# Attention: a step's weighing is issued behind all four scores and maxima of the next step

## The chip, the cores and the metric

The kernel runs on one core of one Trainium2 chip. The metric is the device time of one execution in microseconds (us); the time before is the median of three runs. The engines are TensorE (PE in the profile; PEld are its weight loads), VectorE (DVE), ScalarE (ACT), GpSimd (POOL) and SyncE (SP, which here only issues DMAs).

## The reference

A stack of blocks over x of shape 4 x 1024 x 128: a gated recurrence with a feed-forward part, a mixture of experts, an attention, and an attention with a second mixture of experts. This case is about the two attentions, which compute the same with other weights (16 heads of 8 channels, rotary positions, 1024 tokens, 4 batches). The core of the first:

```python
q = _rope(proj(Wq, bq))
k = _rope(proj(Wk, bk))
v = proj(Wv, bv)
...
scores = jnp.einsum('bhtd,bhsd->bhts', q, k) / scale
attn = jax.nn.softmax(scores, axis=-1)
out = jnp.einsum('bhts,bhsd->bhtd', attn, v)
out = out.transpose(0, 2, 1, 3).reshape(Bb, Tt, C)
return jnp.einsum('btc,oc->bto', out, Wo) + bo
```

## The kernel before

The program is a row of stages; within a stage every engine has its own list of instructions, written by hand, and the engines meet only in semaphores. `attention` is one such stage and is called twice (layer 0 and layer 1).

**Groups and steps.** Four heads of one batch make a group; there are 16 groups. A group has 16 steps: two halves h of 512 query columns, and 8 blocks i of 128 keys for each half. So a layer has 256 steps, the kernel 512. Four names recur below.

- *Score* (`score(s, j)`, line 956): keys x queries of head j in step s, one matmul of 64 rows by 512 columns into one of three PSUM banks (`NS = 3`). It waits until ScalarE has taken the exponent of the score three before it (`exped`). Score 2 of a step thus waits for exponent 3 of the step before, and score 3 for exponent 0 of its own step; score 0 waits for exponent 1 and score 1 for exponent 2 of the step before.
- *Exponent* (line 1019, ScalarE): reads the bank, writes `p`, 128 x 512. `p` has room for three steps.
- *Weighing* (`weigh(s)`, line 966): the four `p` of step s times the values `v_ext`, summed over the 8 key blocks in the PSUM bank `O_BANK`. It waits for all four exponents of its step. The program has four matmuls, which the trace shows as 8 records.
- *Maximum* (`fill` of kind "max", line 922 on TensorE, line 1039 on VectorE): the softmax maxima are found 12 steps ahead. Each is a matmul into one of four PSUM banks (`NM = 4`, a ring) and a reduction by VectorE. A step has four of them; `more(todo)` issues one behind each score. The last 12 steps of a layer have none.

Heads 0 and 1 lie in the lower 64 rows of the array and heads 2 and 3 in the upper; the maxima are ordered so that a score and the maximum behind it use different rows, and the two run side by side. The names "pair" below mean such a score and its maximum.

**What else goes into a step.** `fill_plan` puts rarer work at the end of some steps (`for f in todo`). It shares the ring of four banks: "turn_max" (line 926, transposes the maxima of a half so that they can be stored into row 24 of `qs`, once in 8 steps), "turn_out" (line 931, transposes a finished output, once in 8 steps; VectorE divides it, lines 1054 and 1058), and "turn_o" and "project" (lines 938 and 944, two of each once in 64 steps). When a half is finished, in the first step behind it, ScalarE copies `O_BANK` to `o_raw` (`copy_out`, line 1003) between exponent 2 and exponent 3; it waits for the last weighing of the half (`weighed`), and the next half's first weighing waits for it (`out_copied`).

Of the kernel before, what the change touches and what calls it, by code (L numbers as in the profile page):

```python
# [848 lines left out]
def attention(nc, t, w, layer, a):  # L849
# [14 lines left out]
    with stage(nc, "loaded0", "loaded1", "loaded2", "loaded3", "row0", "row1", "filled", "used", "turned",  # L864
# [34 lines left out]
        def _(pe):  # L899
# [48 lines left out]
            def score(s, j):  # L948
                g, (h, i) = s // STEPS, divmod(s % STEPS, NT)
                n = GH * s + j  # L950
                if i == 0 and j == 0:
                    pe.wait_ge(row[h], 16 * (g + 1))
                if n >= NS:
                    pe.wait_ge(exped, n - NS + 1)
                r = slice(j // KM * KT, (j // KM + 1) * KT)
                pe.matmul(psum[:, S_BANK + n % NS, :], a["ks"][r, g % NKF, j % KM, i * P:(i + 1) * P],  # L956
                          a["qs"][r, g % NKF, h * HALF:(h + 1) * HALF], start=True, stop=True).then_inc(scored, 1)

            def weigh(s):
                g, (h, i) = s // STEPS, divmod(s % STEPS, NT)  # L960
                b, h0 = g // NG, (g % NG) * GH
                pe.wait_ge(exped, GH * (s + 1))
                if i == 0 and (g or h):
                    pe.wait_ge(out_copied, NH * g + h)
                for j in range(GH):
                    last = pe.matmul(psum[GR * j:GR * j + VW, O_BANK, :], t["v_ext"][:, b * NT + i, VE * (h0 + j):VE * (h0 + j) + VW],  # L966
                                     a["p"][:, (GH * s + j) % NP, :], start=(i == 0), stop=(i == NT - 1))
                last.then_inc(weighed, 1)

            def more(todo):  # L970
                if todo and todo[0][0] == "max":
                    fill(todo.pop(0))
# [5 lines left out]
            for s in range(nsteps):  # L978
                todo = list(plan[s])
                score(s, 0)  # L980
                more(todo)
                score(s, 1)
                more(todo)
                if s:
                    weigh(s - 1)
                score(s, 2)
                more(todo)
                score(s, 3)
                more(todo)
                for f in todo:  # L990
                    fill(f)
            weigh(nsteps - 1)
# [380 lines left out]
```

## Time and profile before

| | us |
|---|---|
| median of three runs | 2863.93 (2863.02 to 2864.11) |
| profiled execution, its own time | 2837.83 |
| profiled execution, span | 2836.5 |
| TensorE busy | 2165.7 (76%) |
| VectorE busy | 2123.1 (75%) |
| ScalarE busy | 1456.9 (51%) |
| mean granted TensorE clock over the span | 0.872 |

The span is what lies between the first and the last instruction of the trace. A granted clock of 1.00 is 2.4 GHz, 0.50 is 1.2 GHz. The attention stages take two stretches of the span, whose first scores start at 837 us and at 1717 us and which end at about 1558 us and 2437 us.

### The profile page before, as it was taken

What the parts mean: (1) busy time and instruction counts of PE and PEld (TensorE: products, weight loads), DVE (VectorE), ACT (ScalarE), POOL (GpSimd) and SP (SyncE); (2) the same over time, 40 slices, a digit from 0 to 9 for tenths busy, and PEclk for the clock granted to TensorE, in tenths of its full rate; (3) what the DMA queues carried; (4) which work ended last, traced back from release to release, by engine and by line L of the source; (5) the groups of instructions that cost most, each with busy time, mean ns of one, the idle gap of its engine ahead of it and who ended that gap; (6) DMA issues with size and microseconds to landing.
All of it is one profiled execution on the core that took longest, in us unless ns stands there. A gap on an engine that the chain in (4) does not pass through costs nothing. (4 is left out here: it accounts for less than half of the span.)

```text
span 2836.5 us, 39102 instructions
## 1 busy us (share of the span) xinstructions
PE 2165.7 (76%) x13128; PEld 1149.2 (41%) x13128; DVE 2123.1 (75%) x4605; ACT 1456.9 (51%) x2898; POOL 504.2 (18%) x410
## 2 busy tenths in 40 slices
PE   6888955853279999999998559999999999449920
PEld 5667744741133333333332323333333333249910
DVE  6667657644569999999994668999999998375635
ACT  4443430421017777777777106777777777304510
POOL 2223300756600000000000330000000000005644
PEclk9989965986659999999999768999999999758965
DMA  4000000342320000000000330000000000202211
GB/s 171 0 0 0 0 29 8 91 89 84 101 80 25 15 23 24 13 25 13 25 1 1 104 124 13 24 13 25 24 13 24 13 13 2 89 15 60 68 46 52
DMA packets 64544, 109.19 MB, mean 38 GB/s; under 512 B 10352, under 2 KB 44272, under 8 KB 64112
## 3 DMA queue, kind: packets, MB, share of 16 engines
q1 hardware_dynamic: 55408, 88.60, 9.2%
q0 software_dynamic: 8960, 18.37, 2.9%
q8 instruction: 95, 1.56, 0.2%
q14 instruction: 81, 0.66, 0.1%
HBM read 64.46 MB, written 41.94 MB: 38 GB/s over the span
## 5 line engine op out<-in xcount | busy, mean ns | idle before, releaser
L1039 DVE TENSOR_REDUCE mh<-psum 128x1 f32<-128x512 f32 x2048 | 1276.0, 684 | 135.8 <-PE psum L922 121.1
L1019 ACT ACTIVATE p<-psum 128x512 f32<-128x512 f32 x2048 | 1072.9, 603 | 331.3 <-PE psum L956 331.3
L956 PE MATMUL psum<-qs,ks 64*128 64x512 f32 x2048 | 750.0, 449 | 88.7 <-ACT p L1019 88.7
L922 PE MATMUL psum<-ks,qs 64*128 64x512 f32 x2048 | 775.1, 464 | 35.0 <-DMA ks<-qk_parts 34.3
L956 PEld LDWEIGHTS psum<-qs,ks 64*128 64x128 f32 x2048 | 331.4, 185 | 714.9 <-ACT p L1019 695.5
L966 PE MATMUL psum<-p,v_ext 128*32 128x512 f32 x4096 | 548.0, 607 | 31.7 <-ACT p L1019 31.7
L922 PEld LDWEIGHTS psum<-ks,qs 64*128 64x128 f32 x2048 | 342.0, 190 | 79.3 <-DMA ks<-qk_parts 34.7
L157 PE MATMUL psum<-ident,xn 128*128 128x128 f32 x160 | 44.4, 455 | 262.1 <-DVE xn L125 218.2
L575 ACT ACTIVATE hid<-psum,stage 128x128 f32<-128x128 f32 x448 | 132.5, 367 | 181.2 <-PE psum L545 181.2
L519 POOL DMA_INDIRECT x_in<-n_rows,token_of x152 | 167.4, 1102 | 250.7 <-POOLq L78 183.7
L966 PEld LDWEIGHTS psum<-p,v_ext 128*32 128x32 f32 x4096 | 81.0, 108 | 188.4 <-ACT p L1019 184.1
L649 POOL COPY n_all<-xn 128x1024 f32 x4 | 4.2, 1040 | 829.0 <-DVE xn L132 829.0
L615 POOL DMA_INDIRECT back<-answers,slot_of x128 | 132.8, 1038 | 100.1 <-issue 51.7
L1265 POOL MEMSET v_ext<- 128x5344 f32 x2 | 9.1, 4551 | 788.8 <-POOLq L78 788.8
L598 DVE COPY stage<-ew 128x642 f32 (+1 forms) x152 | 96.0, 631 | 69.0 <-DVE y_out L590 63.8
L545 PE MATMUL psum<-x_t,stage 128*128 128x128 f32 x896 | 137.1, 290 | 9.3 <-DVE x_t L584 6.3
L157 PEld LDWEIGHTS psum<-ident,xn 128*128 128x128 f32 x160 | 29.4, 191 | 273.9 <-DVE xn L125 222.1
L555 PE MATMUL psum<-stage,hid 128*128 128x128 f32 x896 | 126.3, 277 | 0.6 <-ACT hid L575 0.6
L545 PEld LDWEIGHTS psum<-x_t,stage 128*128 128x128 f32 x896 | 114.2, 195 | 25.7 <-DVE x_t L584 23.9
L229 PE MATMUL psum<-y_high,w_high 128*128 128x512 f32 x256 | 106.6, 416 | 20.3 <-PEq L78 20.3
L138 ACT ACTIVATE std<-var 128x8 f32<-128x8 f32 (+1 forms) x29 | 6.1, 210 | 211.3 <-DVE var L110 187.2
L555 PEld LDWEIGHTS psum<-stage,hid 128*128 128x128 f32 x896 | 113.6, 194 | 1.0 <-ACT hid L575 1.0
(172 smaller groups left out, 2405.8 us busy)
## 6 DMA issues: line engine op xcount, KB each, us to landing
qs<-qk_parts SPq DMA_DIRECT2D x128, 100.0 KB
ks<-qk_parts SPq DMA_DIRECT2D x128, 100.0 KB
answers<-y_out SPq DMA_DIRECT2D x152, 64.0 KB, 1.5
qk_parts<-qh SPq DMA_DIRECT2D x16, 512.0 KB, 4.4
qk_parts<-kh SPq DMA_DIRECT2D x16, 512.0 KB, 4.3
ew<-in_moe SPq DMA_DIRECT2D x1, 5136.0 KB, 18.1
ew<-in_moe SPq DMA_DIRECT2D x1, 4624.0 KB, 13.9
n_rows<-xn SPq DMA_DIRECT2D x8, 512.0 KB, 3.2
```

Of the source, the lines that this page charges most:

```text
L229: last = pe.matmul(psum[:, n % BANKS, :], a[:, m, c * P:(c + 1) * P], t[y][:, h * HALF:(h + 1) * HALF], start=(k == 0), stop=(k == 2))
L519: pool.indirect_dma_start(t["x_in"][:, i % NX, :], None, t["n_rows"], bass.IndirectOffsetOnAxis(ap=t["token_of"][:, i:i + 1], axis=0))\
L545: last = pe.matmul(psum[:, 2 + i % 2, f * P:(f + 1) * P], t["stage"][:, i % NST, W1 + f * P:W1 + (f + 1) * P], t["x_t"][:, i % 2, :], star ...
L555: last = pe.matmul(psum[:, 4 + i % 2, 0:P], t["hid"][:, i % 2, f, :], t["stage"][:, i % NST, W2 + f * P:W2 + (f + 1) * P], start=(f == 0), ...
L575: act.activation(t["hid"][:, i % 2, f, :], psum[:, 2 + i % 2, f * P:(f + 1) * P], func, bias=t["stage"][:, i % NST, B1 + f:B1 + f + 1]).th ...
L598: dve.tensor_copy(t["stage"][:, i % NST, :], t["ew"][:, bass.ds(e, 1), :] .rearrange("p a c -> p (a c)")).then_inc(staged, 1)
L615: pool.indirect_dma_start(t["back"][:, b % 2, i, k, :], None, t["answers"], bass.IndirectOffsetOnAxis(ap=t["slot_of"][:, b * NT + i, k:k + ...
L922: pe.matmul(psum[:, bank, :], a["qs"][r, g % NKF, i * P:(i + 1) * P], a["ks"][r, g % NKF, j % KM, k * HALF:(k + 1) * HALF], start=True, st ...
L956: pe.matmul(psum[:, S_BANK + n % NS, :], a["ks"][r, g % NKF, j % KM, i * P:(i + 1) * P], a["qs"][r, g % NKF, h * HALF:(h + 1) * HALF], sta ...
L966: last = pe.matmul(psum[GR * j:GR * j + VW, O_BANK, :], t["v_ext"][:, b * NT + i, VE * (h0 + j):VE * (h0 + j) + VW], a["p"][:, (GH * s + j ...
L1019: act.activation(a["p"][:, n % NP, :], psum[:, S_BANK + n % NS, :], ACT.Exp, scale=DH ** -0.5)\
L1039: dve.tensor_reduce(a["mh"][:, g % 2, c, k:k + 1], psum[:, bank, :], AX.X, ALU.max).then_inc(used, 1)
```

## The change

The weighing of the step before is issued behind the fourth score and the fourth maximum of a step, and ahead of the rarer work at its end; before it stood behind the second maximum.

```diff
             for s in range(nsteps):
                 todo = list(plan[s])
                 score(s, 0)
                 more(todo)
                 score(s, 1)
                 more(todo)
-                if s:
-                    weigh(s - 1)
                 score(s, 2)
                 more(todo)
                 score(s, 3)
                 more(todo)
+                if s:
+                    weigh(s - 1)
                 for f in todo:
                     fill(f)
             weigh(nsteps - 1)
```

Only TensorE's list changes. In a step with a "turn_out" (L931) at its end, TensorE's list was (L956 is a score, L922 a maximum, L966 a weighing):

```order
 L956 MATMUL psum<-qs_1,ks_1 128x512
 L922 MATMUL psum<-ks_1,qs_1 128x512
 L966 MATMUL psum<-p_1,v_ext_1 32x512 x4
 L956 MATMUL psum<-qs_1,ks_1 128x512
 L922 MATMUL psum<-ks_1,qs_1 128x512
 L956 MATMUL psum<-qs_1,ks_1 128x512
 L922 MATMUL psum<-ks_1,qs_1 128x512
 L931 MATMUL psum<-ident_1,o_raw_1 128x128 x4
 L956 MATMUL psum<-qs_1,ks_1 128x512
```

The first two rows are the step's second pair, the last is the first score of the next step. At the same place TensorE's list now is:

```order
 L956 MATMUL psum<-qs_1,ks_1 128x512
 L922 MATMUL psum<-ks_1,qs_1 128x512
 L956 MATMUL psum<-qs_1,ks_1 128x512
 L922 MATMUL psum<-ks_1,qs_1 128x512
 L956 MATMUL psum<-qs_1,ks_1 128x512
 L922 MATMUL psum<-ks_1,qs_1 128x512
 L966 MATMUL psum<-p_1,v_ext_1 32x512 x4
 L931 MATMUL psum<-ident_1,o_raw_1 128x128 x4
 L956 MATMUL psum<-qs_1,ks_1 128x512
```

The weighing has moved behind two more pairs, and now stands right ahead of the turned output, with no score between the two. At a "turn_max" (L926), TensorE's list before was, from the third pair of its step to the second pair of the next and its weighing:

```order
 L956 MATMUL psum<-qs_1,ks_1 128x512
 L922 MATMUL psum<-ks_1,qs_1 128x512
 L956 MATMUL psum<-qs_1,ks_1 128x512
 L922 MATMUL psum<-ks_1,qs_1 128x512
 L926 MATMUL psum<-ident_1,mx_1 16x128
 L956 MATMUL psum<-qs_1,ks_1 128x512
 L922 MATMUL psum<-ks_1,qs_1 128x512
 L956 MATMUL psum<-qs_1,ks_1 128x512
 L922 MATMUL psum<-ks_1,qs_1 128x512
 L966 MATMUL psum<-p_1,v_ext_1 32x512 x4
```

Now TensorE has there, from the fourth pair of the same step to the third of the next:

```order
 L956 MATMUL psum<-qs_1,ks_1 128x512
 L922 MATMUL psum<-ks_1,qs_1 128x512
 L966 MATMUL psum<-p_1,v_ext_1 32x512 x4
 L926 MATMUL psum<-ident_1,mx_1 16x128
 L956 MATMUL psum<-qs_1,ks_1 128x512
 L922 MATMUL psum<-ks_1,qs_1 128x512
 L956 MATMUL psum<-qs_1,ks_1 128x512
 L922 MATMUL psum<-ks_1,qs_1 128x512
 L956 MATMUL psum<-qs_1,ks_1 128x512
 L922 MATMUL psum<-ks_1,qs_1 128x512
```

Here too the weighing comes directly ahead of the transpose. The lists of the other four engines are the same as before.

## Rows read from the trace of the kernel before

**Rows 1.** The waits, 850 to 2250 us: who waited for whom, total us, times, longest.

```profile
ACT p L1019 <- PE psum L956: 286.1, 501, 1.7
...
DVE mh L1039 <- PE psum L922: 90.0, 241, 14.2
```

**Rows 2.** Busy time in one stretch of 50 us; PEclk is the granted clock.

```profile
1250.00:1300.00 50.00, 45.97 (x304) 16.33 (x302) 46.70 (x83) 38.47 (x75) 0.00 (x0) 1.00 0.05 18
```

**Rows 3.** The timeline of ScalarE, 1084 to 1094 us: start, us, engine, line, operation.

```profile
1084.51 2.07 ACT L1019 ACTIVATE p<-psum 128x512 f32<-128x512 f32 x4 [0.60 <-PE psum L956]
1087.17 0.60 ACT L1019 ACTIVATE p<-psum 128x512 f32<-128x512 f32 x1 [0.60 <-PE psum L956]
1087.67 0.59 ACT L1003 ACTIVATE o_raw<-psum 128x512 f32<-128x512 f32 x1
1088.14 1.58 ACT L1019 ACTIVATE p<-psum 128x512 f32<-128x512 f32 x3
1090.33 1.08 ACT L1019 ACTIVATE p<-psum 128x512 f32<-128x512 f32 x2 [0.60 <-PE psum L956]
...
1093.24 1.09 ACT L1019 ACTIVATE p<-psum 128x512 f32<-128x512 f32 x2 [0.52 <-PE psum L956]
```

**Rows 4.** The timeline of TensorE over the same steps, 1087 to 1092 us.

```profile
1087.82 0.49 PE L956 MATMUL psum<-qs,ks 64*128 64x512 f32 x1 [0.22 <-ACT p L1019]
...
1088.80 1.07 PE L966 MATMUL psum<-p,v_ext 128*32 128x512 f32 x8 [0.48 <-ACT p L1019]
1089.80 0.50 PE L956 MATMUL psum<-qs,ks 64*128 64x512 f32 x1
...
1090.13 0.39 PE L956 MATMUL psum<-qs,ks 64*128 64x512 f32 x1
...
1090.46 0.66 PE L931 MATMUL psum<-ident,o_raw 128*128 128x128 f32 x4
1091.05 0.49 PE L956 MATMUL psum<-qs,ks 64*128 64x512 f32 x1
...
1091.38 0.39 PE L956 MATMUL psum<-qs,ks 64*128 64x512 f32 x1
...
1091.71 1.07 PE L966 MATMUL psum<-p,v_ext 128*32 128x512 f32 x8
```

**Rows 5.** The timeline around a "turn_max", 1302 to 1306 us, TensorE and ScalarE.

```profile
1303.04 0.28 PE L926 MATMUL psum<-ident,mx 128*16 128x128 f32 x1
1303.25 0.50 PE L956 MATMUL psum<-qs,ks 64*128 64x512 f32 x1
...
1303.70 0.50 PE L922 MATMUL psum<-ks,qs 64*128 64x512 f32 x1
1304.13 1.07 PE L966 MATMUL psum<-p,v_ext 128*32 128x512 f32 x8
...
1302.92 2.06 ACT L1019 ACTIVATE p<-psum 128x512 f32<-128x512 f32 x4 [0.61 <-PE psum L956]
1305.65 0.60 ACT L1019 ACTIVATE p<-psum 128x512 f32<-128x512 f32 x1 [0.67 <-PE psum L956]
```

**Rows 6.** The timeline of VectorE: two ends of one period of 8 steps.

```profile
1068.22 1.29 DVE L1039 TENSOR_REDUCE mh<-psum 128x1 f32<-128x512 f32 x2 [0.67 <-PE psum L922]
...
1090.37 1.29 DVE L1039 TENSOR_REDUCE mh<-psum 128x1 f32<-128x512 f32 x2 [0.67 <-PE psum L922]
...
1092.06 3.70 DVE L1039 TENSOR_REDUCE mh<-psum 128x1 f32<-128x512 f32 x6
```

**Rows 7.** The timeline at the end of layer 1: the last weighing and its copy.

```profile
2433.89 1.07 PE L966 MATMUL psum<-p,v_ext 128*32 128x512 f32 x8 [0.94 <-ACT p L1019]
2435.02 0.60 ACT L1003 ACTIVATE o_raw<-psum 128x512 f32<-128x512 f32 x1 [1.19 <-PE psum L966]
```

**Rows 8.** The timeline of TensorE: the two "turn_o" and the two "project" of a batch.

```profile
1027.23 1.09 PE L938 MATMUL psum<-ident,x 128*128 128x128 f32 x8
...
1033.25 2.05 PE L944 MATMUL psum<-att,y_t 128*128 128x128 f32 x16
```

## The prediction

> **What bounds the kernel now.** I read the page first. The change touches TensorE's list in the two attentions alone, so everything outside them is left as it is. Of the attentions I read the waits, then the busy time by stretches, and then the timelines, because no engine is full: in [rows 2] TensorE is busy for 45.97 of 50 us, VectorE for 46.70, ScalarE for 38.47, at the full clock. The reader should see that three engines are near the bound and none is on it. The longest wait is ScalarE's for scores, 286.1 us in 501 waits [rows 1]; VectorE waits 90.0 us for maxima. So it is a ring of waits between ScalarE and TensorE that sets the pace, and I have to find it and then find the ring that takes its place.
>
> The ring before, from [rows 3, 4]. Exponent 2 starts; exponent 3 starts 0.49 us later (four take 2.07, one takes 0.60, so (2.07 - 0.60) / 3 = 0.49). It lasts 0.60. TensorE goes on 0.05 after an exponent's end (1087.17 + 0.60 = 1087.77, score at 1087.82). What goes on is the weighing, which holds TensorE for 1.00 (1088.80 to 1089.80); behind it stands score 2, and the exponent that it feeds starts 0.53 after it (1089.80 to 1090.33). The sum is 0.49 + 0.60 + 0.05 + 1.00 + 0.53 = 2.67 us a step. A plain step took 2.66 (1084.51 to 1087.17). The ring explains the pace to 0.01.
>
> Three kinds of step are longer. Measured between exponents 2, the step with the copy of the output takes 1090.33 - 1087.17 = 3.16, 0.49 more. The one with "turn_out" takes 1093.24 - 1090.33 = 2.91, 0.24 more. The one with "turn_max" takes 1305.65 - 1302.92 = 2.73, 0.07 more [rows 5]. A period of 8 steps has one of each: 8 x 2.67 + 0.80 = 22.16; VectorE's timeline has 22.15 between two equal places [rows 6].
>
> **The change part by part.** Nothing is added or removed.
>
> *The plain step.* The weighing leaves the way of score 2. But it then stands behind score 3, and score 3 waits for exponent 0 of its own step (three banks). Score 0 of the next step stands behind the weighing and feeds the next exponent 0. So there is a new ring: exponent 0 lasts 0.60; 0.05 to score 3; from score 3 to the start of the weighing a time x; the weighing 1.00; score 0 to exponent 0 0.53. That is 2.18 + x. For x the trace has these rows. Where a weighing followed such a matmul and did not wait for ScalarE, it came 0.43 later (1303.70 to 1304.13) [rows 4, 5]. Score 3 will have waited, so I take 0.43; the bounds are 0.33 and 0.49, the latter being the most that any wait for the next exponent leaves between a score and a weighing, as exponents come 0.49 apart. The step becomes 2.61, the ring having lost 0.49 and gained 0.43: 0.06 a step, over 512 steps -31 us.
>
> *The copy of the output* now waits for a weighing that is issued late in its own step, and exponent 3 stands behind the copy on ScalarE. The copy starts 1.13 after the start of its weighing (2433.89 to 2435.02) [rows 7], exponent 3 0.47 later (1087.67 to 1088.14), and the next exponent 0 0.49 behind that: 2.09 after the weighing's start, against 1.53 in a plain step. The step is longer by 0.56, before by 0.49. That is 0.07 for each of 62: +4 us. The last copy of each layer is behind the loop.
>
> *"turn_out"* now stands between the weighing and score 0, and both are in the ring. It holds TensorE for 0.59 (1090.46 to 1091.05) [rows 4]. Before, it stood between score 3 and the next score 0, where TensorE waited for ScalarE anyway (0.22 before a score in [rows 4]), and cost 0.24. The cover is gone: +0.35 for each of 62, +22 us. This is the term that eats the gain.
>
> *"turn_max"* holds TensorE for 0.21 (1303.04 to 1303.25) [rows 5] and cost 0.07: +0.14 for each of 62, +9 us. Its maxima were merged two steps earlier, and the DMA of its row still has more than two steps before the score that needs it, so no wait appears there.
>
> *"turn_o" and "project"* (1.09 and 2.05 us in [rows 8], 6 places each) lose at most the same cover of 0.35: +4 us.
>
> *The ends.* The last weighing of a layer no longer waits behind exponents 2 and 3 in a row as the ring had it, about 0.7 earlier in each layer. Together -1 us.
>
> *VectorE* needs per period 32 maxima at 0.60 ((3.70 - 0.68) / 5 = 0.604 [rows 6], one reduction taking 0.68) and about 0.5 more for the turned output (1090.37 + 1.21 = 1091.58, next maximum at 1092.06) and at most that for each of the other two extras: 19.3 + 1.5 = 20.8 at most. That is under 22, so it stays off the path. A maximum waits for the reduction four before it. Counted from score 0 of a plain new step, the first reduction starts at about 0.57, the fourth at 2.38, and it ends at 3.06; the next step's score 3 goes at 2.61 + 0.53 + 0.60 + 0.05 = 3.79. So the bank is free 0.7 us before it is wanted, and VectorE may be late by that.
>
> Sum: -31 + 4 + 22 + 9 + 4 - 1 = +7 by these rounded terms. The first one hangs on 0.49 - 0.43, two numbers each read to 0.01, and 0.01 is 5 us. With the ring closed on the longer average (22.15 for a period before; after, 8 x 2.605 + 0.56 + 0.59 + 0.21 = 22.20, 62 periods, and the +3 of the other two parts) it is +6. I take +5, as half-hidden turns can only be cheaper than fully shown ones. The profiled execution's own time was 2837.83 with a span of 2836.5; I expect a span near 2842. The median of the runs lies 26 us above that execution, and I carry the difference over: 2864 + 5 = 2869.
>
> **The rivals.** Of what a measurement can tell, 0.2% is 5.7 us.
>
> *The ring closes tighter (faster).* If the weighing's weights go in while score 3 still streams, x is 0.33, and the step loses 0.16 rather than 0.06: 51 us less than my forecast, 2818. For it: the 0.33 of [rows 4]. Against: that pair had not waited.
>
> *The ring falls away and VectorE becomes the bound (faster by far).* This is the plain reading of the waits: scores no longer stand behind the weighing, ScalarE's 286 us go, VectorE runs without a gap. A period would be 20.5 rather than 22.15; 62 of them save 102 us: 2762. Against: it needs score 0 not to stand behind a weighing that stands behind score 3.
>
> *VectorE holds the fourth maximum (slower).* The weighing now stands behind four maxima rather than two. If the ring of four banks makes maximum 3 wait, the weighing and all behind it wait. In [rows 5] a maximum came 0.11 behind its score. 0.11 in every step is +56 on top: 2925. It decides once VectorE is more than 0.7 late in most steps; its extras of 0.5 a piece do not reach that alone.
>
> *The clock falls (slower).* TensorE's idle time is gathered at another place of the step. At 1.2 GHz its parts of the ring (0.43 + 1.00 + 0.53) double at most, 1.96 more a step; one step in twenty would give +50: 2919. For it nothing in [rows 2], where the clock is 1.00 with the same work spread over 2% more time. The Trainium skill (TensorE: Matmul & The Clock Gate, A second HAM failure mode: psum-queue depth-cycling) says that a kernel which idles briefly between matmul groups while cycling PSUM banks swings between the two levels; this kernel does just that already, and the row shows no swing.
>
> The Trainium skill (TensorEngine Tiling, Key Properties) also says that changing the tiling mode drains the engine. Every weighing is such a change in both orders, and by that rule alone "turn_out" behind a weighing saves one change; the rows' 0.59 for it holds whatever drain there is.
>
> **How the numbers follow.** Forecast (the ring through score 3, near balance): 0.70, of which 0.33 within 0.2%, 0.33 slower and 0.04 faster; its own range is 2858 to 2880. Tighter ring 0.10. VectorE the bound 0.05. VectorE holds the fourth maximum 0.08. Clock 0.07. Faster: 0.04 + 0.10 + 0.05 = 0.19. Within: 0.33, and 0.02 for mild forms of the two slower rivals: 0.35. Slower: 0.33 + 0.13 = 0.46. The range is that of the forecast, widened by x from 0.41 to 0.47 (0.02 of x is 10 us): 2850 to 2893.
>
> **What would show it.** Right: plain steps of 2.61 between exponents 0, and score 3 of each step 0.05 behind the end of exponent 0; the weighing 0.43 behind score 3; ScalarE idle ahead of exponent 0 instead of exponent 2, by about 0.6; the step with "turn_out" longer by 0.59; the copy about 1.13 behind its weighing. Wrong: a weighing at 0.33 behind score 3, plain steps under 2.55, reductions without gaps, a granted clock under 1.00 in the middle of a layer, or maxima that lag their scores.

## The result and the profile after

The changed kernel takes 2897.01 us (median of four runs, 2895.31 to 2908.82) against 2864.02: a ratio of 1.0125, with an interval of 1.0097 to 1.0152. It is slower by 33 us where +5 was forecast, and lies 4 us above the upper end of the range.

The profiled execution has a span of 2894.2 us, 58 more than the one of before. Not all of that is the change's. From the first score to the end of the last weighing, layer 0 took 720.3 us before and takes 735.9, layer 1 took 718.3 and takes 736.2: together 1438.6 and 1472.1, +33.5. The other 24 us lie outside the attentions, in stages whose code is the same (1397.9 and 1422.1); a second run of the changed kernel, below, has 1397.7 there. The kernel before was profiled in an execution 26 us below its median (2837.83 and 2863.93), the changed kernel in one at its median; so the medians seem to hold these 24 us on both sides, and the number to explain is the +33 inside the attentions. What sets the 24 us is not shown. In what follows "attentions" is this sum over both layers, from the first and last records of each.

The waits of the changed kernel, 850 to 2250 us (who waited for whom, total, times, longest), against [rows 1]; the last line is the kernel before:

```profile
ACT p L1019 <- PE psum L956: 275.8, 369, 2.7
...
DVE mh L1039 <- PE psum L922: 79.3, 285, 14.3
DVE rs L1054 <- PE psum L931: 67.6, 53, 17.9
...
DVE rs L1054 <- PE psum L931: 31.8, 2, 20.1
```

ScalarE waits for scores about as long as before, in fewer and longer waits. VectorE, which hardly ever waited for a turned output (2 times), now does so 53 times. The busy time in the same 50 us as [rows 2]:

```profile
1250.00:1300.00 50.00, 44.25 (x296) 15.59 (x288) 46.05 (x80) 37.48 (x73) 0.00 (x0) 1.00 0.08 29
```

The granted clock is 1.00 as before, so it was not the clock. Each engine is a little less busy. The timeline of ScalarE, which answers to [rows 3] (start, us, engine, line, operation, what it waited for):

```profile
1293.69 2.07 ACT L1019 ACTIVATE p<-psum 128x512 f32<-128x512 f32 x4 [0.61 <-PE psum L956]
1296.36 1.57 ACT L1019 ACTIVATE p<-psum 128x512 f32<-128x512 f32 x3 [0.61 <-PE psum L956]
1298.57 0.60 ACT L1003 ACTIVATE o_raw<-psum 128x512 f32<-128x512 f32 x1 [0.64 <-PE psum L966]
1299.07 2.55 ACT L1019 ACTIVATE p<-psum 128x512 f32<-128x512 f32 x5
1302.80 2.07 ACT L1019 ACTIVATE p<-psum 128x512 f32<-128x512 f32 x4 [1.18 <-PE psum L956]
1305.47 2.07 ACT L1019 ACTIVATE p<-psum 128x512 f32<-128x512 f32 x4 [0.60 <-PE psum L956]
```

ScalarE now idles ahead of exponent 0, as forecast. But a plain step is 1296.36 - 1293.69 = 2.67, not 2.61. The copy waits 0.64 for its weighing, and the step with the turned output ends in a wait of 1.18. The timeline of TensorE over the last two steps, against [rows 4]:

```profile
1300.20 0.49 PE L956 MATMUL psum<-qs,ks 64*128 64x512 f32 x1
...
1300.63 1.06 PE L966 MATMUL psum<-p,v_ext 128*32 128x512 f32 x8
1301.62 0.66 PE L931 MATMUL psum<-ident,o_raw 128*128 128x128 f32 x4
1302.21 0.49 PE L956 MATMUL psum<-qs,ks 64*128 64x512 f32 x1
...
1303.45 0.49 PE L956 MATMUL psum<-qs,ks 64*128 64x512 f32 x1 [0.28 <-ACT p L1019]
1303.45 0.49 PE L922 MATMUL psum<-ks,qs 64*128 64x512 f32 x1
...
1303.87 1.07 PE L966 MATMUL psum<-p,v_ext 128*32 128x512 f32 x8
1304.87 0.50 PE L956 MATMUL psum<-qs,ks 64*128 64x512 f32 x1
```

Four of the five parts of the forecast ring can be read off. Exponent 0 starts at 1302.80 and lasts 0.60, and score 3 goes at 1303.45, 0.05 after its end. The weighing comes 0.42 behind score 3 and holds TensorE for 1.00 (1303.87 to 1304.87). The fifth is off: exponent 0 starts 0.60 behind score 0 (1304.87 to 1305.47; 1302.21 to 1302.80 is 0.59), where score 2 was followed by exponent 2 after 0.53 in [rows 3, 4]. So the new ring is 0.06 longer than I made it, and just as long as the old one.

The turned output holds TensorE for 0.59 (1301.62 to 1302.21), as forecast, and here nothing covers it.

### The profile page after: what moved, and what is told of

It reads as the page before. It is cut to its first block and busy times, and to the rows that moved or that the text cites. A ratio compares the mean times of both kernels' runs of the same rounds, so it can differ in the third digit from the quotient of the medians.

```text
span 2894.2 us, 39102 instructions
## 1 busy us (share of the span) xinstructions
PE 2157.0 (75%) x13128; PEld 1149.3 (40%) x13128; DVE 2131.9 (74%) x4605; ACT 1449.3 (50%) x2898; POOL 504.8 (17%) x410
## 5 line engine op out<-in xcount | busy, mean ns | idle before, releaser
L1019 ACT ACTIVATE p<-psum 128x512 f32<-128x512 f32 x2048 | 1057.0, 604 | 328.8 <-PE psum L956 328.8
L956 PE MATMUL psum<-qs,ks 64*128 64x512 f32 x2048 | 761.1, 450 | 163.6 <-ACT p L1019 163.6
L922 PE MATMUL psum<-ks,qs 64*128 64x512 f32 x2048 | 781.9, 466 | 35.1 <-DMA ks<-qk_parts 34.4
L956 PEld LDWEIGHTS psum<-qs,ks 64*128 64x128 f32 x2048 | 336.9, 185 | 745.6 <-ACT p L1019 670.3
L966 PE MATMUL psum<-p,v_ext 128*32 128x512 f32 x4096 | 547.4, 606 | 0.0
L922 PEld LDWEIGHTS psum<-ks,qs 64*128 64x128 f32 x2048 | 347.9, 190 | 85.6 <-DMA ks<-qk_parts 34.8
L966 PEld LDWEIGHTS psum<-p,v_ext 128*32 128x32 f32 x4096 | 80.9, 108 | 124.8 <-issue 68.9
```

Of the source, the lines that this page charges most:

```text
L922: pe.matmul(psum[:, bank, :], a["qs"][r, g % NKF, i * P:(i + 1) * P], a["ks"][r, g % NKF, j % KM, k * HALF:(k + 1) * HALF], start=True, st ...
L1019: act.activation(a["p"][:, n % NP, :], psum[:, S_BANK + n % NS, :], ACT.Exp, scale=DH ** -0.5)\
```

## The experiments

**The changed kernel again**, for the chip on which most experiments ran.

> The changed kernel itself, unedited, on the chip of these runs, so that the edits stand against it under the same conditions. The two attentions 1472 us as in its first trace; the kernel about 33 us slower than the kernel before; what lies outside the attentions as in the kernel before of the same chip.

It took 2873.39 us against 2837.69 for the kernel before on that chip: 1.0125, interval 1.0106 to 1.0143, the same ratio as first measured. Attentions 1471.1 us, the rest of the span 1397.7.

**Where do the 0.06 us come from?** Exponent 0 differs from the other exponents by a second wait in the text. The raw records of the trace show how the two are carried: a semaphore instruction of 17 ns at line 1018 holds the wait that is written last, the one for the score, and the exponent itself the one written first, for the weighing. The exponent starts 62 ns behind that instruction (median). In the kernel before, where ScalarE is still busy with exponent 3 at that point, the same distance is 30 ns, and the pair costs nothing that shows. Two runs put it to the test, one in each kernel. The first, in the changed kernel, takes it off the path by exchanging the order:

```diff
-                    if j == 0 and s >= NP // GH:
-                        act.wait_ge(weighed, s - NP // GH + 1)
                     act.wait_ge(scored, n + 1)
+                    if j == 0 and s >= NP // GH:
+                        act.wait_ge(weighed, s - NP // GH + 1)
```

> The changed kernel, with one edit on ScalarE: exponent 0 waits for its score first and for the weighing of three steps before second (the two waits are the same, only their order in the text is exchanged). In the changed kernel score 0 is followed by exponent 0 after 0.60 us, where the same step before the change took 0.53 for score 2 and exponent 2; exponent 0 alone has two waits. Theory A (the second wait costs 0.06 us when ScalarE arrives at it idle, because the blocking wait stands in an instruction of its own): score 0 to exponent 0 falls to 0.53, plain steps from 2.665 to 2.605, each attention about 15 us shorter, the kernel about 31 us faster than the changed one, near 2866. Rival B (the 0.06 belongs to score 0, its bank or its place behind the weighing): nothing changes, 2897.

It took 2846.35 us against 2839.55 on its chip, 1.0018 (1.0007 to 1.0029), where the changed kernel has 1.0125. Attentions 1445.5, 26 less than the changed kernel's and 7 more than the kernel before. Its timeline, ScalarE and then TensorE:

```profile
1301.80 2.06 ACT L1019 ACTIVATE p<-psum 128x512 f32<-128x512 f32 x4 [0.55 <-PE psum L956]
1304.41 2.07 ACT L1019 ACTIVATE p<-psum 128x512 f32<-128x512 f32 x4 [0.55 <-PE psum L956]
...
1302.45 0.50 PE L956 MATMUL psum<-qs,ks 64*128 64x512 f32 x1 [0.22 <-ACT p L1019]
...
1302.88 1.07 PE L966 MATMUL psum<-p,v_ext 128*32 128x512 f32 x8
1303.88 0.50 PE L956 MATMUL psum<-qs,ks 64*128 64x512 f32 x1
```

Score 0 at 1303.88, exponent 0 at 1304.41: 0.53. The plain step is 2.61, the number of the prediction. So are the +7: with this wait out of the way, the kernel does what the prediction's own sum (+7) says of the changed one. The second run does the reverse in the kernel before, where exponent 2 is the one that ScalarE idles for:

```diff
-                    if j == 0 and s >= NP // GH:
+                    if j in (0, 2) and s >= NP // GH:
                         act.wait_ge(weighed, s - NP // GH + 1)
```

> The kernel before, with the wait for the weighing of three steps before put ahead of exponent 2 as well as exponent 0. It is always met by then, so it holds nothing up by itself. Theory A (a second wait ahead of the exponent that ScalarE idles for costs 0.06 us): score 2 to exponent 2 grows from 0.53 to 0.60, plain steps from 2.667 to 2.73, the kernel +31 us, near 2895. Rival B (the 0.06 belongs to score 0): no change, 2864.

It took 2867.56 us, 1.0096 (1.0070 to 1.0122). Its timeline, TensorE and then ScalarE:

```profile
1302.67 0.49 PE L956 MATMUL psum<-qs,ks 64*128 64x512 f32 x1
...
1303.27 2.07 ACT L1019 ACTIVATE p<-psum 128x512 f32<-128x512 f32 x4 [0.57 <-PE psum L956]
...
1305.99 1.57 ACT L1019 ACTIVATE p<-psum 128x512 f32<-128x512 f32 x3 [0.66 <-PE psum L956]
```

Score 2 to exponent 2 is now 0.60 and the step 2.72 to 2.73. A wait that was met long before makes the kernel 28 us slower, because it makes the wait that does block an instruction of its own. Not all of that is the 0.06. Attentions 1471.8, 33 more than before, but some 9 of these us lie in the last six steps of layer 1, which ran at half clock (0.50 from 2445 to 2465 us). The steps alone give about 24: the ones with the turned output and the turned maxima did not grow. The rival, that the 0.06 belongs to score 0 or its bank, falls.

The control is the exchanged order in the kernel before, where exponent 0 is not waited for:

> The kernel before with only the order of exponent 0's two waits exchanged. There exponent 0 follows exponent 3 without idle time, so its second wait lies under the exponent before it. Theory: no change, the two attentions 1439 us as before, within 3 us. Rival (the order of the waits is worth something by itself): up to 30 us less.

One run, 2845.92 us. Layer 1 took 718.5 us, as before; plain steps stay 2.67. Layer 0 took 728.8, 8.5 more, so the attentions come to 1447.3, 8 over the 1439 that I expected within 3. The surplus lies in the last steps of that layer. The busy time there, first this run, then the kernel before:

```profile
1545.00:1555.00 10.00, 9.48 (x35) 2.47 (x27) 0.00 (x0) 4.15 (x8) 0.00 (x0) 0.50 0.00 0
...
1545.00:1555.00 10.00, 8.19 (x46) 2.25 (x45) 0.00 (x0) 8.20 (x16) 0.00 (x0) 1.00 0.00 0
```

The granted clock was 0.50 from about 1538 us to the layer's end at 1566, and a step there took 4.07 us; in the kernel before it was 1.00 in the same stretch, and a step 2.67. Layer 1 of this same run kept 1.00 to its end, so the surplus does not follow from the order of the waits. What sets it, this single run does not show.

**The turned output and maxima.** In the changed kernel they stand between the weighing and score 0. This run issues them behind the third maximum, ahead of score 3, where TensorE idles; `fill_plan` lists them one place earlier, so VectorE's list follows.

```diff
                 score(s, 2)
                 more(todo)
+                while todo and todo[0][0] != "max":
+                    fill(todo.pop(0))
                 score(s, 3)
```

> The changed kernel, with the rarer work of a step (turned maxima and outputs, turn_o, project) issued behind the third maximum, ahead of score 3, rather than behind the weighing. Theory A (in the new order this work lost its cover because it stands between the weighing and score 0; ahead of score 3 TensorE idles by about 0.3 us anyway): the step with a turned output falls from +0.59 over a plain step to about +0.3, the one with turned maxima from +0.21 to about 0, so about 0.5 us a period of 8 steps, about 30 us in all: near 2867. Rival (the cost is TensorE's own time, wherever it stands, since it is in the ring either way): 2897.

It took 2866.87 us (1.0109, 1.0067 to 1.0151), but its four runs lie far apart, from 2851.77 to 2879.54, and by the median alone it could not be told from the changed kernel (1.0125). The trace is of the lowest. In it the attentions take 1457.0: 15 less than the changed kernel, half of what I expected, and the steps say where. The step with the turned maxima fell from 2.88 to 2.74, all its cost but 0.07. The one with the turned output fell only from 3.26 to 3.20. Its timeline (the functions stand four lines lower, so L960 is the score and L935 the turned output):

```profile
1296.17 0.50 PE L960 MATMUL psum<-qs,ks 64*128 64x512 f32 x1 [0.55 <-ACT p L1025]
...
1296.60 0.66 PE L935 MATMUL psum<-ident,o_raw 128*128 128x128 f32 x4
1297.19 0.50 PE L960 MATMUL psum<-qs,ks 64*128 64x512 f32 x1
```

Score 2 waits 0.55 for exponent 3, which the copy has made late in the step before. The idle time lies ahead of score 2 instead of score 3, so the cover is not where the work stands.

**The copy.** ScalarE's copy goes behind exponent 3.

```diff
-                    if j == 2 and s and s % NT == 0:
+                    if j == 3 and s and s % NT == 0:
```

> The changed kernel, with ScalarE's copy of the finished output behind exponent 3 rather than ahead of it. Theory A (exponents 3 and 0 stand behind a copy that waits for a weighing issued late): the step with the copy falls from +0.51 to about +0.1 over a plain step, as the copy then starts as soon as its weighing ends and holds only exponent 0 for about 0.1; 62 copies, about 25 us faster than the changed kernel, near 2872. Rival (the next weighing, which waits for the copy, becomes late): no gain or a loss.

It took 2843.08 us, 1.0012 (1.0002 to 1.0022); attentions 1441.8, 30 less than the changed kernel, where I expected 25. The timeline at a copy:

```profile
1290.16 2.07 ACT L1019 ACTIVATE p<-psum 128x512 f32<-128x512 f32 x4 [0.60 <-PE psum L956]
1292.37 0.60 ACT L1003 ACTIVATE o_raw<-psum 128x512 f32<-128x512 f32 x1
1292.87 2.06 ACT L1019 ACTIVATE p<-psum 128x512 f32<-128x512 f32 x4
1296.12 2.06 ACT L1019 ACTIVATE p<-psum 128x512 f32<-128x512 f32 x4 [1.19 <-PE psum L956]
```

The step with the copy is 1292.87 - 1290.16 = 2.71, 0.04 over a plain one; the 0.51 is gone. The next, with the turned output, still has its 0.58.

**Both together**, to see whether the cover comes back once the copy is out of the way:

> The changed kernel with the copy behind exponent 3 and the rarer work ahead of score 3, and exponent 0's waits as they were. Alone, the earlier rare work took only 0.06 from the step with the turned output (0.59 to 0.54), since that step still began late from the copy. Theory: with the copy out of the way its step is 0.2 to 0.35 over a plain one, the copy's step 0.04 over, plain steps stay at 2.667; the two attentions together 1472 - 30 - 15 - 15 = 1412 to 1420 us. Rival: the turned output costs 0.5 wherever it stands.

One run, 2803.26 us. Attentions 1405.9, 66 less than the first trace of the changed kernel, where the two edits alone give 15 and 30. The step with the turned output is 2.87, 0.21 over a plain one, and the one with the copy 2.70. The 21 us beyond the sum are the cover: the step with the turned output fell by 0.39, where the two edits alone had taken 0.06 together.

**All three.**

> The changed kernel with all three edits: the order of exponent 0's two waits exchanged, the rarer work ahead of score 3, and the copy of the output behind exponent 3. If the ring through exponent 0, score 3, weighing, score 0 is what sets the pace, the edits add: plain steps 2.61, the copy's step about 2.65, the turned maxima's 2.68, the turned output's 2.61 plus about 0.3 (with the copy no longer late, score 2 is early again and the cover is back): a period of 8 steps of 21.3 to 21.4 against 22.15 before, each attention 25 us shorter than before, the kernel about 50 us faster than the kernel before, near 2790. Rival: VectorE, which needs at most 20.8 a period, or the ring of four banks for the maxima becomes the bound first: plain steps stay above 2.63, the gain is under 30 us.

It took 2780.07 us against 2837.69: 0.9795 (0.9779 to 0.9810), the fastest of all. Attentions 1383.0, 56 less than the kernel before, where I expected about 50. The timeline of ScalarE over the two long steps and two plain ones (six lines lower, L1025 is the exponent, L1009 the copy):

```profile
1290.88 2.06 ACT L1025 ACTIVATE p<-psum 128x512 f32<-128x512 f32 x4 [0.54 <-PE psum L960]
1293.49 2.06 ACT L1025 ACTIVATE p<-psum 128x512 f32<-128x512 f32 x4 [0.55 <-PE psum L960]
1295.70 0.60 ACT L1009 ACTIVATE o_raw<-psum 128x512 f32<-128x512 f32 x1
1296.20 2.06 ACT L1025 ACTIVATE p<-psum 128x512 f32<-128x512 f32 x4
1299.01 2.06 ACT L1025 ACTIVATE p<-psum 128x512 f32<-128x512 f32 x4 [0.75 <-PE psum L960]
1301.62 2.06 ACT L1025 ACTIVATE p<-psum 128x512 f32<-128x512 f32 x4 [0.54 <-PE psum L960]
```

The steps are 2.61, 2.71, 2.81 and 2.61. Since plain steps reach the ring's 2.61, VectorE did not become the bound.

**Is it the ring through score 3?** Four banks for scores and three for maxima free score 3 from exponent 0:

```diff
-S_BANK, NS = 0, 3
-M_BANK, NM = 3, 4
+S_BANK, NS = 0, 4
+M_BANK, NM = 4, 3
```

> The changed kernel with exponent 0's two waits exchanged, and four PSUM banks for scores and three for maxima (it was three and four). Score 3 then waits for exponent 3 of the step before, not for exponent 0 of its own. Theory A (the ring runs through exponent 0 and score 3): score 3 no longer starts 0.05 behind the end of exponent 0, and plain steps fall below the 2.61 of the run with the exchanged waits, to 2.4 to 2.6, where the maxima's three banks or VectorE bound them. Rival (TensorE or VectorE already sets the pace through the place of the weighing): plain steps at 2.61 or above although score 3 is free.

One run, 2857.68 us; it has the exchanged waits too. Attentions 1461.4, 16 more than the same kernel with three score banks. The timeline, TensorE's matmuls and a weight load:

```profile
1103.66 0.62 PE L956 MATMUL psum<-qs,ks 64*128 64x512 f32 x2
1104.39 0.49 PE L922 MATMUL psum<-ks,qs 64*128 64x512 f32 x1
1104.81 1.06 PE L966 MATMUL psum<-p,v_ext 128*32 128x512 f32 x8
...
1104.39 0.18 PEld L922 LDWEIGHTS psum<-ks,qs 64*128 64x128 f32 x1 [0.55 <-DVE mh L1039]
```

Score 3 now streams behind score 2, ahead of exponent 0's end, so that arm of the ring is off. But the fourth maximum waits 0.55 for VectorE with only three banks, and the weighing stands behind it. The plain step is 2.74: the rival of a late VectorE, which four banks had kept away. The expected 2.4 to 2.6 was wrong for these steps. But the last 12 steps of a layer have no maxima, and there the run answers the question. The timeline of ScalarE in the last steps of layer 1, first of this run, then of the one with the exchanged waits and three score banks:

```profile
2443.28 12.18 ACT L1019 ACTIVATE p<-psum 128x512 f32<-128x512 f32 x24 [0.63 <-PE psum L956]
...
2430.07 2.06 ACT L1019 ACTIVATE p<-psum 128x512 f32<-128x512 f32 x4 [0.54 <-PE psum L956]
2432.67 2.06 ACT L1019 ACTIVATE p<-psum 128x512 f32<-128x512 f32 x4 [0.54 <-PE psum L956]
```

With four score banks the 24 exponents of six steps follow one another without a wait, 2.0 us a step (12.18 / 6). With three banks ScalarE waits 0.54 in every step, and the step is 2.60. So it is the ring through score 3 that makes the 2.61. What steps with maxima would be without either ring stays open, since the eight banks do not allow both.

**Another place for the weighing.** It stands ahead of score 3, where TensorE waits for exponent 0:

```diff
+                if s:
+                    weigh(s - 1)
                 score(s, 3)
                 more(todo)
-                if s:
-                    weigh(s - 1)
```

> The changed kernel with the weighing one place earlier: behind the third maximum and ahead of score 3, all else as in the changed kernel. The weighing then fills the time in which score 3 would wait for exponent 0. The ring is: score 2 (waits for exponent 3), third maximum, weighing, score 3, exponent 3: 0.05 + 0.43 + 1.00 + 0.53 + 0.60 = 2.61. Exponent 0 with its two waits, the rarer work at the step's end and most of the copy lie beside it. Theory (what decides is which score stands right behind the weighing and what lies in that ring): plain steps 2.61, the copy's step about 0.1 more, the turned output's 0.2 more, the turned maxima's 0: a period of 21.2 against 22.15, about 58 us faster than the kernel before, near 2780. Rival (the changed place of the weighing costs by itself, however the ring runs): slower than the kernel before.

It took 2790.95 us against 2838.77: 0.9833 (0.9819 to 0.9847), attentions 1392.1. With no other edit this place of the weighing is 48 us faster than the kernel before, and the rival, that moving it costs by itself, falls. Its timeline at a copy, TensorE and ScalarE:

```profile
1101.50 0.50 PE L956 MATMUL psum<-qs,ks 64*128 64x512 f32 x1 [0.22 <-ACT p L1019]
...
1101.93 1.06 PE L966 MATMUL psum<-p,v_ext 128*32 128x512 f32 x8
1102.92 0.50 PE L956 MATMUL psum<-qs,ks 64*128 64x512 f32 x1
...
1100.85 2.06 ACT L1019 ACTIVATE p<-psum 128x512 f32<-128x512 f32 x4 [0.54 <-PE psum L956]
1103.06 0.60 ACT L1003 ACTIVATE o_raw<-psum 128x512 f32<-128x512 f32 x1 [0.15 <-PE psum L966]
1103.56 2.06 ACT L1019 ACTIVATE p<-psum 128x512 f32<-128x512 f32 x4
```

Here the weighing comes 0.43 behind score 2, and exponent 3 is the one waited for, which has a single wait. The copy waits 0.15, its step is 2.71 (1100.85 to 1103.56), and plain ones are 2.61. It fell short of the expected 58 us in the turned output, whose step and the next together cost 0.3 over two plain ones, and in the turned maxima, 0.12 rather than 0.

**The copy in the old order.**

> The kernel before with only the copy of the output put behind exponent 3. There the copy did not wait for its weighing, but held exponent 3, which is in the old ring (exponent 2, exponent 3, weighing, score 2). Theory: behind exponent 3 it holds only exponents 0 and 1 in ScalarE's idle time, the copy's step falls from 3.16 to about 2.67, plain steps stay 2.67: 62 x 0.49 = 30 us faster than the kernel before, near 2808. What the moved weighing is worth beside such a copy is then seen against the run with all three edits (2780). Rival: exponent 1 comes so late that score 0 or 1 of the next step waits, and half of it is lost.

It took 2841.66 us, 1.0007 (0.9997 to 1.0017): nothing gained. TensorE in the copy's step:

```profile
1093.32 0.49 PE L956 MATMUL psum<-qs,ks 64*128 64x512 f32 x1 [0.22 <-ACT p L1019]
...
1094.39 1.07 PE L966 MATMUL psum<-p,v_ext 128*32 128x512 f32 x8 [0.57 <-ACT o_raw L1003]
```

I had overlooked that the next half's first weighing waits for the copy. In the old order that weighing stands behind only two scores and is inside the ring; later by one exponent, the copy holds it back, and its step, between exponents 2, is 3.25 against 3.16 before: longer, not shorter. In the changed order that weighing comes at the end of its step, so there the edit pays.

## Why the prediction was wrong, step by step

- **The old ring** (exponents 2 and 3, weighing, score 2; 2.67): right.
- **The new ring and the plain step, 2.61, -31 us: this term failed.** The ring was the right one and four of its parts have the predicted size, x among them (0.42). (The 0.43 was read from a maximum at 1303.70 in [rows 5] whose score had gone 0.11 earlier; in the new order score 3 and its maximum start together, so the figure held, with some luck.) The part "score 0 to exponent 0 0.53" was taken over from score 2 and exponent 2. It is 0.60, since exponent 0 has two waits and now stands where ScalarE idles. The saving of 0.06 and this 0.06 cancel; the measured term is 0 (plain steps 2.668 and 2.667). Exchanging the waits gave 2.61, and 26 of the 31 us in the attentions' time; the steps with a copy stay at 3.18 with either order. The wait was in the code in front of me, one line above the exponent; I costed no part of the change there because ScalarE's list did not change. What changed was which of its instructions it idles for.
- **"turned output", +0.35 for each of 62, +22:** right; 3.26 against 2.67 for its step, 0.59, and 0.24 before.
- **"turned maxima", +0.14, +9:** right; 2.875 against 2.667, 0.21, and 0.07 before.
- **The copy, +0.07, +4:** the step is 3.18 between exponents 0, 0.51 over a plain one rather than 0.56; +0.02 over before, about +1. This is the same error again: from the weighing to the next exponent 0 it takes 2.10, as forecast (2.09), but in a plain step 1.59 rather than 1.53.
- **"turn_o" and "project", +4:** their steps are 1.07 and 1.88 over such steps without them, before 0.68 and 1.68, so +0.6 for each of six pairs: +4, right.
- **The sum.** With the first term at 0 the others give +22 + 9 + 1 + 4 - 1 = +35. The attentions show +33, the medians +33. The -1 of the ends was not measured by itself.
- **The range.** It allowed x from 0.41 to 0.47, but gave the other parts of the ring nothing. Every 0.01 in any of them is 5 us. It also does not follow from its own rule: 2858 to 2880, widened by 0.02 below and 0.04 above, is 2848 to 2900, not 2850 to 2893. The measured 2897 would lie inside that, for a wrong reason.

The rivals: the clock stayed at 1.00; no maximum lagged its score (score 3 and its maximum both start at 1303.45 in the rows above); the tighter ring and VectorE as the bound did not come.

## What to carry to other kernels

When an edit changes which instruction an engine idles for, cost that instruction as it is written, with all its waits, and not by a sister that looks alike; an extra wait that is always met is free under other work and costs 0.06 us a step where the engine arrives idle, here in a ring that runs 512 times. If two waits stand ahead of an instruction, arrange that the one that blocks is the one the instruction itself carries; in this program that was the one written first. Before moving a block, write down the ring that it leaves and the ring that it enters, and then look which rarer work lies in the new one: here that work, which holds TensorE for 0.2 and 0.6 us once each in 8 steps, was nearly the whole loss, and one place earlier for the same block was worth 48 us.

## What the runs showed of the hardware

- Two executions of the changed kernel differed by 24 us outside the attentions, in the same code. Whether that is the chip or the execution is not shown.
